# A decoder layer on one core: all engines reordered, attention's chain spread over two steps, one product for the positions

## The reference

```python
x = x + self_attention(layernorm(x))        # q, k with rotary positions; causal mask; softmax
x = x + cross_attention(layernorm(x), ctx)  # 77 keys, no mask
# feed-forward on h = layernorm(x):
shared = (h @ sup * silu(h @ sgate)) @ sdown
e      = argmax(h @ router_w)               # 8 logits; experts 0..6 exist, 7 has none
x = x + 2 * softmax_top * expert_e(h) + shared
```

## Time and profile before

| | us |
|---|---|
| median of 3 runs | 1129.05 |
| lowest, highest | 1126.96, 1132.03 |
| span of the profiled execution | 1100.5 |
| first stage: first work of PE to the last count of experts | about 15 to 878 |
| second stage | about 887 to 1100 |

### The profile page before, as it was taken

The page is one execution under the profiler, slowest core; times in us unless marked ns, Lnnn a source line. Parts: engine busy times, 40 slices in busy tenths (PEclk is TensorE's granted clock), DMA queues, the critical chain, the costliest instruction groups (busy, mean ns, idle before and its releaser), DMA issues.

```text
span 1100.5 us, 50361 instructions
## 1 busy us (share of the span) xinstructions
PE 1043.7 (95%) x16352; PEld 890.1 (81%) x16353; DVE 858.9 (78%) x2853; ACT 732.1 (67%) x1557; POOL 629.3 (57%) x1488
## 2 busy tenths in 40 slices
PE   2789999999999999999999999999999879999995
PEld 2567888888888888888888888888887879999995
DVE  3358888888888888888888888888886447777774
ACT  0367777777777777777777777777775235555552
POOL 0345666666666666666666666666664314444443
PEclk9799999999999999999999999999999989999998
DMA  5132111011011000110001110111100032222220
GB/s 102 37 101 73 57 30 37 27 25 25 25 34 26 25 25 25 33 27 25 25 25 33 27 25 25 25 33 28 28 23 26 27 91 63 74 70 69 70 68 5
DMA packets 66668, 44.50 MB, mean 40 GB/s; under 512 B 24135, under 2 KB 61451, under 8 KB 66592
## 3 DMA queue, kind: packets, MB, share of 16 engines
q1 hardware_dynamic: 55424, 30.35, 10.7%
q0 software_dynamic: 5312, 12.18, 3.3%
q10 hardware_dynamic: 5856, 0.99, 0.7%
HBM read 23.96 MB, written 18.29 MB: 38 GB/s over the span
## 4 chain that ended last, share of the span: by engine, by line
PE 88%; issue 2%; POOL 2%; DVE 1%; ACT 1%; DMA 0%; SPq 0%; POOLq 0%; DVEq 0%; ACTq 0%
PE pv L1190 11%; PE scores L1077 6%; PE scores L1374 6%; PE scores L1232 6%; PE scores L1379 6%; PE ro L1391 6%; PE scores L1239 5%; PE ro L1247 5%; PE st L1302 5%; PE pj L1213 4%; PE scores L1111 4%; PE ro L1207 3%; PE ro L1199 3%; PE scores L1103 3%; PE ro L1287 3%
## 5 line engine op out<-in xcount | busy, mean ns | idle before, releaser
L992 ACT ACTIVATE arena<-scores 128x1024 f32<-128x1024 f32 (+1 forms) x256 | 261.9, 1024 | 55.3 <-PE scores L1111 49.1
L669 DVE TENSOR_REDUCE arena<-scores 128x8 f16<-128x1024 f32 (+1 forms) x256 | 254.5, 994 | 25.3 <-PE scores L1085 14.8
L914 ACT ACTIVATE arena<-st 128x128 f16<-128x128 f16 (+2 forms) x256 | 155.1, 606 | 23.8 <-PE st L1324 14.6
L1190 PE MATMUL pv<-arena 128*32 128x128 f32 (+1 forms) x4096 | 139.8, 278 | 0.3 <-ACT arena L992 0.3
L449 POOL TENSOR_TENSOR arena<-arena,neg_half 128x1 f32<-128x1 f32 x192 | 107.5, 560 | 28.7 <-POOL arena L440 10.5
L1190 PEld LDWEIGHTS pv<-arena 128*32 128x32 f32 (+1 forms) x4096 | 105.0, 110 | 15.1 <-ACT arena L992 0.8
L676 DVE STREAM_TRANSPOSE arena<-pv 128x256 f32<-128x256 f32 x128 | 57.0, 445 | 47.8 <-PE pv L1190 47.7
L914 ACT ACTIVATE arena<-arena 128x512 f16<-128x512 f32 (+2 forms) x192 | 92.5, 482 | 2.5 <-DVE arena L710 1.4
L550 POOL DMA_INDIRECT out_dram<-x_tile x70 | 69.5, 992 | 39.0 <-POOL carried L549 26.6
L1077 PEld LDWEIGHTS scores<-causal 32*128 32x128 bf16 x2048 | 47.3, 92 | 54.2 <-issue 52.7
L440 POOL TENSOR_TENSOR arena<-arena,eps 128x1 f32<-128x1 f32 x192 | 36.6, 190 | 81.6 <-DVE arena L651 81.6
(11 more groups left out here) (175 smaller groups left out, 2804.6 us busy)
## 6 DMA issues: line engine op xcount, KB each, us to landing
x_tile<-xs SPq DMA_DIRECT2D x70, 129.0 KB, 2.1
arena<-arena SPq DMA_DIRECT2D x512, 4.0 KB
arena<-in_x_dram SPq DMA_DIRECT2D x64, 64.0 KB, 2.2
out_dram<-pay SPq DMA_DIRECT2D x64, 64.0 KB, 2.2
arena<-in_ctx_dram SPq DMA_DIRECT2D x64, 38.5 KB
w_gate<-in_L_ffn_gate_w_dram SPq DMA_DIRECT2D x7, 256.0 KB, 2.7
w_up<-in_L_ffn_up_w_dram SPq DMA_DIRECT2D x7, 256.0 KB, 3.0
w_down<-in_L_ffn_down_w_dram SPq DMA_DIRECT2D x7, 256.0 KB, 4.0
```

The costliest lines, as they stand in the source:

```text
L669: v.tensor_reduce(nmax[:, n, :].rearrange("p (m r s) -> p r m s", r=2, s=SLOT)[:, u, :, 0:HG], pair(s)[:, :, 0:HG * keys].rearrange("p m ( ...
L914: return a.activation(to, of, ACT.Copy)
L992: a.activation(e32[0:rows, 2 * n + u, :], scores[0:rows, 1024 * s:1024 * (s + 1)], ACT.Exp).then_inc(sexp_done[n][u], 1)
L1190: last = t.matmul(pv[SLOT * j:SLOT * (j + 1), 0:2 * P].rearrange("p (c a y) -> p a c y", a=2, y=SLOT)[:, a], vals[0:rows, p, at0:at0 + SLO ...
```

## The change

Every `step` function of the first stage has another order and other lags; LAG goes from 15 to 13. The pieces themselves are the same but for these parts (the row bank's users and the tuples of `turn` are written anew to fit the order):

```diff
@@ score buffer of the shared expert is an argument now (DVE, ACT); it becomes s = 0
-            def half_of(b, p):
+            def half_of(b, p, s):
...
-scores[:, 1024 * 1:1024 * 1 + F]
+scores[:, 1024 * s:1024 * s + F]
@@ PE
+            def self_for_exp(b, p, u, s, now, *before):
+
+                wait(pe, max_rows[0][p], 32 * b + 64 - 32 * p)
+                turn(pe, b, now, *before)
+                for h in range(4):
+                    mask_round(s, u, 1, h)
+                for g in range(HG):
+                    self_exp_round(s, u, p, g)
...
-                for n, before_in in enumerate((earlier, ones16)):
-                    cols = ro[:, 2 * P + n * E:2 * P + (n + 1) * E]
-                    t.matmul(cols, before_in[:, :], hot16[:, p, :], start=True, stop=False)
-                    last = t.matmul(cols, id32[:, :], run_base[:, :], start=False, stop=True)
+                cols = ro[:, 2 * P:2 * P + 2 * E].rearrange("p (n e) -> p n e", n=2)
+                t.matmul(cols, id32[:, :], run_base[:, :].unsqueeze(1).to_broadcast([P, 2, E]), start=True, stop=False,
+                         skip_group_check=True)
+                t.matmul(cols[:, 0], earlier[:, :], hot16[:, p, :], start=False, stop=False, skip_group_check=True)
+                last = t.matmul(cols[:, 1], ones16[:, :], hot16[:, p, :], start=False, stop=True, skip_group_check=True)
...
-                two_turns(i, p, self_exp, 6, 0, 1, ..., self_exp, 6, 1, 0, ...)
+                two_turns(i, p, self_exp, 4, 1, 1, ..., cross_max, 6, 0, 0, ...)
+                at(i, p, 6, cross_for_max, 1, 0, ...)
+                at(i, p, 4, self_for_exp, 0, 1, ...)
...
+                at(i, p, 3, self_for_max, 0, 0, ...)
+                at(i, p, 3, self_for_max, 1, 1, ...)
```

More of the change, by code:

```diff
@@ L395, in step @@
             def step(i, p):
[L396 to L400, removed]
+                at(i, p, 4, load_x)
+                at(i, p, 9, rows_of_max, 1)
+                at(i, p, 13, base_out)
+                at(i, p, 6, rows_of_max, 0)
+                at(i, p, 6, load_ctx)
             def step_and_weights(i, p):
@@ L788, in step @@
             def step(i, p):
[L789 to L821, removed]
+                at(i, p, 6, row_max, 1, 1, 0)
+                at(i, p, 7, turned, 1)
+                at(i, p, 5, ln_mean_var, 1)
+                at(i, p, 2, rope_products)
@@ new lines, in step @@
+                at(i, p, 3, row_max, 0, 0, 0)
+                at(i, p, 3, row_max, 0, 1, 1)
+                at(i, p, 5, q2_bias)
+                at(i, p, 7, recip, 1)
+                at(i, p, 1, ln_stats_of, 0)
+                at(i, p, 4, turned, 0)
+                at(i, p, 7, turned_back, 1)
+                at(i, p, 9, put_of)
+                at(i, p, 4, recip, 0)
+                at(i, p, 9, gate_of)
+                at(i, p, 9, add_shared)
+                at(i, p, 8, half_of, 0)
+                at(i, p, 1, ln_mean_var, 0)
@@ new lines, in step @@
+                at(i, p, 7, add_cross)
+                at(i, p, 7, ln_stats_of, 2)
+                at(i, p, 4, turned_back, 0)
+                at(i, p, 8, hidden_of, 0)
+                at(i, p, 8, logits_copy)
+                at(i, p, 7, ln_mean_var, 2)
+                at(i, p, 8, top_of)
+                at(i, p, 8, marks_of)
+                at(i, p, 4, add_attention)
+                at(i, p, 8, mark_top_of)
+                at(i, p, 4, ln_stats_of, 1)
+                at(i, p, 8, hot_of)
@@ L822, in _ @@
+                at(i, p, 5, row_max, 1, 0, 0)
+                at(i, p, 4, k2_bias)
+                at(i, p, 8, hot_pos_of)
+                at(i, p, 8, run_of)
             run(dve, step)
@@ L1002, in step @@
             def step(i, p):
[L1003 to L1022, removed]
+                at(i, p, 4, qkT_copy)
+                at(i, p, 5, exps, 0, 1, 1)
+                at(i, p, 6, values2_in)
+                at(i, p, 9, xn3_out)
+                at(i, p, 5, exps, 0, 0, 1)
+                at(i, p, 10, router_exp)
+                at(i, p, 9, xT_copy, 2)
+                at(i, p, 7, nmT_copy, 1)
+                at(i, p, 6, xT_copy, 1)
+                at(i, p, 6, k2_high)
+                at(i, p, 3, values_in)
+                at(i, p, 3, qk_high)
+                at(i, p, 6, q2_high)
+                at(i, p, 4, nmT_copy, 0)
+                at(i, p, 5, ctxT_copy)
+                at(i, p, 9, tanh_of, 0)
+                at(i, p, 7, exps, 1, 0, 1)
+                at(i, p, 6, qkT2_copy)
+                at(i, p, 2, xT_copy, 0)
+                at(i, p, 7, exps, 1, 1, 1)
             run(act, step)
@@ L1326, in step @@
             def step(i, p):
[L1327 to L1330, removed]
@@ new lines, in step @@
+                two_turns(i, p, self_exp, 4, 1, 1, (((sexp_done[1][1], -2),), ((sexp_done[1][0], -2),), ((smax_done[0][1], 1),), ((sexp_done[0][0], 0),), ((sexp_done[0][1], 0),),),
+                          cross_max, 6, 0, 0, (((sh_hid, -2),), ((smax_done[0][0], 3),), ((smax_done[1][1], 0),), ((smax_done[1][0], 0),),))
+                at(i, p, 7, values, 1, ((o_turned[0], 3),), ((o_turned[1], 0),))
+                at(i, p, 9, positions, ((resid_done[0], 5),), ((logits_ready, 1),), ((resid_done[1], 2),), ((sh_added, 0),), ((q2_ready, 4),), ((xT_ready[1], 4),), ((xT_ready[2], 1),), ((hot_posed, 0), (run_ready, 0)))
```

98 lines of the change are left out of this document (49 added, 49 removed).

## The result

In the first measurement before took 1129.68 us (median of 4 runs, three of them the ones that the forecast started from) and after 1112.33 (4 runs, 1107.18 to 1115.36): ratio 0.9837, 95% interval 0.9814 to 0.9861. The forecast was 1109 us, range 1090 to 1127. But later measurements (on chips called 9, 0 and 2 here) gave another picture. Before then had a median of 1100.3 to 1101.2 us in each of four sets (71 runs in all), and after, run again in one of these sets, took 1099.91 (12 runs) beside before at 1100.3: ratio 1.0005, 0.9988 to 1.0022. So the gain of 1.6% was not a property of the kernels alone. Both findings need an account, and the second is the cleaner one, since there traces of both exist.

A forecast was written before the change was run, and what follows sets the result against it. PE's own list bounds the kernel at 12.51 us a step; a ring over the cross maxima would take over at 12.30. Span 1100.5 - 11.5 (steady) - 6 (fill) - 2 (drain) = 1081, time about 1109 us, range 1090 to 1127.

The forecast's parts named there:

- The runs' median lies 28.55 us over the span of the profiled execution, and what lies around it isn't changed: Whole kernel: step from the forecast span of 1081 us to the time, 1129 - 19.5, about 1109 us.
- if the ends lose what the steps gain: Sign of being wrong: pipeline fill and drain lose what the steady steps gain; the other was a period over 12.5.
- Positions: PE's list: four float32 and two float16 matmuls become two and two; -0.21 us a step, bounds -0.23 and -0.15.
- only there can the step be shortened: Steady step: the period is PE's own list, unless a ring through other engines is as long.
- Scores: PE's list: eight score halves reordered, 2.93 to 2.78 us, -0.15 a step, bounds +0.32 and -0.25.
- so 0.17 of it is a wait: PE's old order: of the 0.32 us piece right behind `hidden_of`, 0.17 is waiting to read the score buffer.
- Array-mode changes (full, strips, columns) are 12 before and 13 now: PE's list: one more mode change, about 0.1 us, cancelling the 0.1 us a step saved on small waits.
- Neighbours: PE's score halves in different strips overlap: pairs at 0.85, 0.63 and 0.60 us; rival that they save nothing, chance 0.03.
- The ring: Cross maxima's way through ACT's copy, SP's transfers and PE: sets the period at 12.3 us, bounds 12.15 and 12.5; chance 0.45.
- I take -2 for the whole drain, bounds -8 and +4: Pipeline's end: 2 us less in all, though the shared expert's last product comes about 1.5 us later.
- Other engines "at nothing": New orders of DVE, ACT and POOL cost nothing more, PE's list covering them; each 0.1 us sticking out is 5.5 us.
- The fill, -6: Pipeline's start: about 7.3 steps instead of 8 from `xT 0` to `positions`; -6 us, bounds -12 and +3.

The follow-up runs named there:

- k11_ctx: The kernel before with one short piece, `ctxT_of`, moved ahead of the cross max half behind `shared_up`, old product for positions: 1108.1 us, ratio to before 1.0071.
- k7_after: The changed kernel run again without any edit, beside new runs of before: 1099.91 us against 1100.3; its second profile is of a 1098.56 us execution.
- k0_before: The kernel before, unchanged, run again for a second profile: 1101.13 us (median of 10 runs), period 12.52 us.
- k4_rotnm: The changed kernel with DVE's list begun six items later and ACT's `nmT_copy, 1` moved ahead of `router_exp` and `xT_copy, 2`: 1089.56 us, ratio to before 0.9900.
- after: The changed kernel, unedited; here the trace of its profiled execution in the first measurement, 1115.36 us.
- k2_rot: The changed kernel with DVE's list begun six items later, in the same cyclic order: 1094.03 us, ratio to before 0.9925.

## Why the prediction was right, and why less than it seems

**The time came out right (1112.33 in 1090 to 1127), by a step that is false.** "The runs' median lies 28.55 us over the span of the profiled execution, and what lies around it isn't changed" took a difference between two executions for a cost around one. The time is the span + 1.8 to 2.3 us in every run with a recorded span. The profile was of an execution that took about 1102.4, the timed ones took 1127 to 1132. From 1102.4 my sum gives 1083, where after takes 1099.9: a forecast of -19.5 us for -0.4. Under the first measurement's conditions it was -17.4, but after's trace there has late signals of PE and a period longer than before's 12.52, so the agreement is luck and no support for the terms.

The prediction's own sign of being wrong, "if the ends lose what the steps gain", is what the second profiles show: steady -7.0 us, drain +8.0.

**Positions: right in size (-0.21 forecast, 0.22 and 0.23 measured), right only through the order.** That it would be worth this in the old order, too, as "only there can the step be shortened" implied, was wrong.

**Scores: right mechanism, gain undersized at first sight.** Pairs of 0.83, 0.57 and 0.55 for 0.85, 0.63 and 0.60. The sum of 2.64 against 2.93 is -0.29, forecast -0.15. But with -0.23 for positions the list should then be 12.00, and it is 12.23 once DVE's turn is cured. What is missing I read, piece by piece in the same chains, mostly as changes of mode, each charged to the piece behind it (read and not tested): `qkv` (0.84 for 0.65), `stacks2` (0.47 for 0.36), the router (0.32 for 0.23), the two output products (0.65 for 0.50) and `positions` itself (0.11 less, start to start, for 0.23 of work) are 0.66 dearer; `ctxT`, `xT 2`, `stacks` and the shared expert's first two products 0.57 cheaper; the first cross exp half, `xT 1` and `values 0` take some 0.2 more. "Array-mode changes (full, strips, columns) are 12 before and 13 now" counted them; it should have gone through the list piece by piece. For the old 0.32, "so 0.17 of it is a wait" was wrong by most of it: `k11_ctx`, without the wait, still has 0.25.

**Neighbours: right.** The rule of the Trainium skill weighed in the prediction ("TensorE: Matmul & The Clock Gate", Part 3, "The mechanism", matmuls strictly in program order) does not describe these traces: at 580.20 to 580.24 masks of another strip start between cross products, and parting a pair cost 0.38 us, some 0.26 of it for the lost overlap by the sum above.

**The ring: the right one, in the wrong place.** At 12.3 it was to bind the steady part. There it only touches: with ACT's copy 0.55 us earlier the period is the same 12.23. The measured 12.35 lies near the forecast's 12.3 by luck: it is PE's list at 12.23 and DVE's turn. The ring stands in the drain, where a chain of `k7_after` reads:

```profile
828.60 0.30 ACT rexp L931 x2
828.90 0.09 ACT arena L913
...
829.05 0.28 ACT arena L913
...
829.34 0.66 SPq L391
...
831.41 1.83 DMA arena<-arena
...
833.27 0.42 PE scores L1110 x8
```

This is the ring as forecast, link by link: exponential, `router_exp`, two copies, the issues, the landing, the cross half. "I take -2 for the whole drain, bounds -8 and +4" failed: +8.0. The new order puts the cross maximum and the cross exp half only one step apart, so that a draining step, no longer filled by PE's work, becomes as long as this chain. That is read from the chains and no run shows it by itself. The counts bear it out in part. The four intervals behind the sixth of the drain's twelve are 12.9, 11.8, 11.2 and 10.6 us in after, and the chain holds SP's issues and the landing there; they are 11.7, 10.5, 8.6 and 8.6 in before (`k0_before`), with no transfer of maxima in the chain: +7.0. The last two intervals are 14.3 for 12.5, with the shared expert's products in the chain and no transfer: +1.8. The first six give back 0.9. And only the stretch from `nmT 1` to the cross half counts, 4.4 us: in the last two long steps ACT's exponential is not in the chain, and `k4_rotnm`, whose copy is 0.55 us earlier, drains in 134.0 us for 134.5.

**Other engines "at nothing": wrong by 0.12 us a step,** the turn of DVE's loop. A list's head is a place with a price, and the forecast did not ask which piece stood there.

**The fill, -6: at most half of it seen.** In the second profiles the first count is 1.5 us later. Over all traces it comes at 109.0 us on average in the nine of the new order (106.4 to 111.7) and at 111.7 in the five of the old one (109.4 to 113.0): -2.7, with ranges that overlap.

## What to carry to other kernels

Take work from an engine only after asking what else ends level with it: a chain of waits names the last to end, not the one 0.02 us behind, and here a saving of 0.23 us a step was worth 1.1 us in one order and 13.6 us in another. In a written-out order keep the critical chain away from the place where an engine's loop turns, and count the ends of the pipeline as a kernel of their own: their steps are as long as the longest chain, not as the fullest engine. And before a profile carries a forecast, see that its own time is that of the timed runs.

## What the runs showed of the hardware

- Matmuls of different row strips start out of the order of the list, also across pieces (masks at 580.20, cross products ahead of them in the list at 580.24). With a full product between two such halves they took 0.38 us more.
- The turn of a loop on DVE's queue held the next instruction for 0.36 us (`after` and `k7_after`).
- A row transfer of 4 KB held the queue that issued it for 0.64 us on SP and 0.66 on ACT (medians; 0.65 to 0.83 on ACT), where it held up the computing instructions behind it, too.
- A wait of 1.88 us on PE was followed by the lower clock level (0.50 of full speed, 1.2 GHz): `values` went from 1.01 to 1.93 us, and four pieces in sum lost 2.7 us, more than the wait. It is not so each time: 2.01 us without a matmul in the drain of `k7_after` were followed by 1.00, 1.99 us in that of `k2_rot` by 0.50.
- PE's signals reached ACT and DVE 0.5 to 0.8 us late in every second step of the trace of the first occasion, and within 0.05 us in the second trace of the same kernel; the cause is open.
